# Layer norm and row quantisation of a ternary feed-forward, placed in parts within the DVE's loop, with the rounding on ACT

## The reference, cut to what matters

```python
def act_quant(x):                      # per row
    scale = 128 / jnp.clip(jnp.max(jnp.abs(x), axis=-1, keepdims=True), 1e-5)
    xq = jnp.clip(jnp.round(x * scale), -128, 127) / scale
...
gate = bitlinear(x, w_gate)            # act_quant(x) @ ternary(w_gate).T, 512 -> 2048
up = bitlinear(x, w_up)
intermediate = jax.nn.silu(gate) * up
return h_bitlinear(intermediate, w_down)   # act_quant(fwht(intermediate)) @ ternary(w_down).T
...
x = x + jnp.tanh(g_ffn[1]) * _L1_ffn_ref(_layernorm(x, axis=-1), w_gate, w_up, w_down)
```

## Time and profile before

| | us |
|---|---|
| Median of 3 runs | 3520.1 (3517.28 to 3525.03) |
| Profiled execution | 3514.03 |
| Its span, first to last instruction | 3512.3 |
| PE busy | 3126.2 (89%) |
| DVE busy | 2596.9 (74%) |
| ACT busy | 1831.7 (52%) |
| POOL busy | 1416.7 (40%) |

### The profile page before, as it was taken

The page is one execution under the profiler, slowest core; times in us unless marked ns, Lnnn a source line. Parts: engine busy times, 40 slices in busy tenths (PEclk is TensorE's granted clock), DMA queues, the critical chain, the costliest instruction groups (busy, mean ns, idle before and its releaser), DMA issues. The chain is left out here.

```text
span 3512.3 us, 42714 instructions
## 1 busy us (share of the span) xinstructions
PE 3126.2 (89%) x14213; PEld 1828.2 (52%) x14244; DVE 2596.9 (74%) x3478; ACT 1831.7 (52%) x3430; POOL 1416.7 (40%) x957
## 2 busy tenths in 40 slices
PE   7869798999996888799999999999999788998985
PEld 3337554333333555455555555555555366786663
DVE  7865688877765888478777877787778764766886
ACT  5644343666663556465666566656555342664220
POOL 1122278000000000176777677767767544224430
PEclk9879899999998999899999999999999898999997
DMA  3037745222217200254555454445454356675321
GB/s 133 40 124 274 270 113 139 61 59 62 57 30 167 44 1 1 98 175 156 173 175 169 158 173 160 159 159 181 158 171 137 95 196 214 242 258 192 144 72 60
DMA packets 229749, 478.66 MB, mean 136 GB/s; under 512 B 36239, under 2 KB 69647, under 8 KB 213664
## 3 DMA queue, kind: packets, MB, share of 16 engines
q1 hardware_dynamic: 223296, 459.19, 40.6%
q0 software_dynamic: 6240, 16.81, 1.3%
HBM read 387.51 MB, written 92.06 MB: 137 GB/s over the span
## 5 line engine op out<-in xcount | busy, mean ns | idle before, releaser
L2387 POOL TENSOR_TENSOR l2x_inflow<-l2x_dtu,l2x_rows_b 128x512 f32<-128x512 f32 x256 | 420.1, 1641 | 269.3 <-DVE l2x_state L2276 262.7
L178 POOL TENSOR_TENSOR ln_work<-ln_work,minus_half 128x4 f32<-128x4 f32 (+1 forms) x34 | 33.2, 978 | 1016.1 <-DVE ln_work L166 1016.0
L2276 DVE TENSOR_TENSOR_SCAN l2x_state<-l2x_decay,l2x_inflow 128x512 f32<-128x512 f32 x256 | 384.0, 1500 | 17.0 <-ACT l2x_decay L2150 17.0
L1324 DVE TENSOR_REDUCE l1x_mx<-psum 128x2 f32<-128x1024 f32 x256 | 308.2, 1218 | 97.0 <-PE psum L1166 95.4
L2403 POOL TENSOR_TENSOR l2x_y_sum<-l2x_y_sum,l2x_state 128x512 f32<-128x512 f32 x224 | 354.8, 1584 | 33.0 <-DVE l2x_state L2285 33.0
L2085 ACT ACTIVATE l2x_probs<-psum,l2x_soft,l2x_norms 128x512 f32<-128x512 f32 x256 | 195.7, 775 | 319.1 <-DVE l2x_soft L2215 319.1
L1281 ACT ACTIVATE l1x_split<-psum 128x1024 f32<-128x1024 f32 x256 | 262.1, 1025 | 155.7 <-PE psum L1166 155.7
L2285 DVE TENSOR_TENSOR l2x_state<-l2x_state,l2x_rows_c 128x512 f32<-128x512 f32 x256 | 265.7, 1038 | 6.5
L126 PE MATMUL psum<-l2x_probs_t,l2x_v_tok 128*128 128x512 f32 x512 | 237.3, 607 | 29.1 <-ACT l2x_probs_t L212 26.0
L126 PE MATMUL psum<-l2x_xt,l2x_wq 128*128 128x512 f32 x512 | 231.0, 595 | 7.8 <-issue 6.2
L126 PE MATMUL psum<-l2x_kt,l2x_qt 128*128 128x512 f32 x512 | 230.5, 593 | 4.0 <-ACT l2x_probs L2085 4.0
(11 more groups left out here) (459 smaller groups left out, 7202.3 us busy)
## 6 DMA issues: line engine op xcount, KB each, us to landing
l2x_rows_b<-l3x_xd_dram SPq DMA_DIRECT2D x256, 256.0 KB, 3.5
l2x_rows_c<-l3x_xd_dram SPq DMA_DIRECT2D x256, 256.0 KB, 3.6
l2w_raw<-l_w SPq DMA_DIRECT2D x38, 1024.0 KB, 6.2
l2x_wkv<-l2x_kv_dram SPq DMA_DIRECT2D x32, 1024.0 KB, 6.9
l2w_raw<-l_w SPq DMA_DIRECT2D x38, 512.0 KB, 4.6
l1x_heads_dram<-l1x_stage SPq DMA_DIRECT2D x32, 512.0 KB, 3.3
l2x_wq<-l_wq SPq DMA_DIRECT2D x16, 1024.0 KB, 7.0
l2x_wo<-l_wo SPq DMA_DIRECT2D x16, 1024.0 KB, 5.3
```

Source lines behind the costliest of these rows:

```text
L1324: main.drain(dve.tensor_reduce(mx[:, gg % 2, :, j, t], g["psum"][:, b:b + 2, :], AX.X, ALU.max), f"m{n}_0", banks=2)
L2276: dve.tensor_tensor_scan(state[:, s % KEPT, :], decay[:, s % 3, :], inflow[:, s % 3, :], 0.0, ALU.mult, ALU.add).then_inc(scan_done, 1)
L2387: pool.tensor_tensor(inflow[:, s % 3, :], dtu[:], rows_b[:, s % 3, :], ALU.mult).then_inc(inflow_ready, 1)
```

## The change

`LayerNorm.vector` is split in two, `moments` (statistics, up to what POOL needs) and `apply` (the normalised rows). In phase `l1f` the DVE's loop is put in another order: in each step `widest` comes first, then the extra part of that step, then `rest`, `middle` and `down`. `moments` stands in steps 0, 4, 8, 12, `apply` in steps 1, 5, 9, 13, and `quantise_x` in steps 2, 6, 10. `quantise_x` keeps the maximum and the scales; its two passes over the rows leave the DVE. `x_round` on ACT now multiplies each of the four tiles by its row's scale and adds the rounding constant (four passes over 512 columns), waits for these, and then writes `xq` with a Relu of (top - value), which clips above; the copies to `xqt` turn that back (127 minus the value). `x_round` stands ahead of `y_round` in steps 3, 7, 11. The other parts of the program use `vector` as before.

```diff
--- before.py
+++ after.py
@@ -145,8 +145,12 @@
         self.var_ready, self.rstd_ready, self.xn_ready = [sem(name + n) for n in ("_var_ready", "_rstd_ready", "_xn_ready")]
 
     def vector(self, dve, i, batch, xn_free, xn=None, first=0):
+        self.moments(dve, i, batch, first)
+        xn_free()
+        self.apply(dve, i, batch, xn, first)
+
+    def moments(self, dve, i, batch, first=0):
         g, st = self.g, self.steps
-        xn = g["xn"] if xn is None else xn
         st.begin(i)
         part = slice(first, first + self.tiles)
         stats, w = g["ln_stats"][:, part], g["ln_work"][:, :, part]
@@ -164,7 +168,11 @@
         st.wait(dve)
         dve.tensor_scalar(w[:, 5, :], w[:, 4, :], 1.0 / D, LN_EPS, ALU.mult, ALU.add).then_inc(self.var_ready, 1)
         dve.tensor_scalar(w[:, 6, :], w[:, 3, :], 0.5, None, ALU.mult).then_inc(self.var_ready, 1)
-        xn_free()
+
+    def apply(self, dve, i, batch, xn=None, first=0):
+        g, st = self.g, self.steps
+        xn = g["xn"] if xn is None else xn
+        w = g["ln_work"][:, :, first:first + self.tiles]
         dve.wait_ge(self.var_ready, i * 2 + 2)
         dve.wait_ge(self.rstd_ready, i + 1)
         for s in range(self.tiles):
@@ -1511,6 +1519,7 @@
             sem(n) for n in ("had_in", "x_steps", "z_steps", "x_ready", "xq_done", "mid_ready", "y_scale", "y_rounded", "yq_done", "z_in", "scaled")]
         weight_in = [sem(f"weight_in{k}") for k in range(3)]
         empty_made, emptied, top_made = sem("empty_made"), sem("emptied"), sem("top_made")
+        x_rounded = sem("x_rounded")
         ln = LayerNorm(g, sem)
         blk = ph.block()
         weights = [w_gate, w_up, w_down]
@@ -1612,16 +1621,20 @@
 
             def x_round(b):
                 act.wait_ge(x_ready, b + 1)
+                for s in range(ST):
+                    act.activation(tmp[:, s, :], g["xn"][:, s, :], ACT.Copy, scale=xs[:, b % 2, 2, s:s + 1],
+                                   bias=ROUND).then_inc(x_rounded, 1)
+                act.wait_ge(x_rounded, (b + 1) * ST)
                 if b >= 1:
                     ring.wait_filled(act, 0, f"xq{b - 1}_1")
-                act.activation(xq[:].rearrange("p s d -> p (s d)"), tmp[:].rearrange("p s d -> p (s d)"), ACT.Copy,
-                               bias=-ROUND).then_inc(xq_done, 1)
+                act.activation(xq[:].rearrange("p s d -> p (s d)"), tmp[:].rearrange("p s d -> p (s d)"), ACT.Relu,
+                               scale=-1.0, bias=top[:, 0:1]).then_inc(xq_done, 1)
 
             def x_turned(b):
                 for k in range(2):
                     ring.wait_filled(act, 0, f"xq{b}_{k}")
-                    copy(act, "act", ring, f"xq{b}_{k}", xqt[:, b % 2, 2 * k:2 * k + 2, :].rearrange("p c n -> p (c n)"),
-                         bank_bf(f"xq{b}_{k}"))
+                    ring.drain(act.activation(xqt[:, b % 2, 2 * k:2 * k + 2, :].rearrange("p c n -> p (c n)"),
+                                              bank_bf(f"xq{b}_{k}"), ACT.Copy, scale=-1.0, bias=QMAX), f"xq{b}_{k}")
 
             def middle_turned(t):
                 for n in range(4):
@@ -1660,8 +1673,8 @@
                     ring.wait_filled(act, 0, f"ha{t}_{n}")
                     copy(act, "act", ring, f"ha{t}_{n}", half[:, (n - 2) * BLK:(n - 1) * BLK], bank(f"ha{t}_{n}"))
 
+            act.wait_ge(top_made, 1)
             x_round(0)
-            act.wait_ge(top_made, 1)
             for t in range(T1 + 3):
                 if t % ST == 0 and t < T1:
                     x_turned(t // ST)
@@ -1673,10 +1686,10 @@
                     y_turned(t - 3)
                 if 0 <= t - 1 < T1:
                     halves(t - 1)
+                if t % ST == ST - 1 and t // ST + 1 < NB:
+                    x_round(t // ST + 1)
                 if 0 <= t - 2 < T1:
                     y_round(t - 2)
-                if t % ST == ST - 1 and t // ST + 1 < NB:
-                    x_round(t // ST + 1)
 
         @blk.vector
         def _(dve):
@@ -1696,18 +1709,9 @@
                 xst.wait(dve)
                 xst.inc(dve.reciprocal(v[:, 2, :], v[:, 1, :]))
                 xst.wait(dve)
+                dve.sem_inc(x_ready, 1)
                 dve.tensor_scalar(v[:, 4, :], v[:, 1, :], w_abs[:, 0, 0:1], None, ALU.mult).then_inc(scaled, 1)
                 dve.tensor_scalar(v[:, 5, :], v[:, 1, :], w_abs[:, 0, 1:2], None, ALU.mult).then_inc(scaled, 1)
-                if b >= 1:
-                    dve.wait_ge(xq_done, b)
-                for s in range(ST):
-                    xst.inc(dve.tensor_scalar(tmp[:, s, :], g["xn"][:, s, :], v[:, 2, s:s + 1], QMAX, ALU.mult, ALU.min))
-                xst.wait(dve)
-                for s in range(ST - 1):
-                    xst.inc(dve.tensor_scalar(tmp[:, s, :], tmp[:, s, :], QMIN, ROUND, ALU.max, ALU.add))
-                xst.wait(dve)
-                s = ST - 1
-                dve.tensor_scalar(tmp[:, s, :], tmp[:, s, :], QMIN, ROUND, ALU.max, ALU.add).then_inc(x_ready, 1)
 
             def middle(t):
                 b, s = divmod(t, ST)
@@ -1761,21 +1765,25 @@
 
             quantise_x(0)
             for t in range(T1 + 3):
+                b = t // ST
                 if 0 <= t - 2 < T1:
                     widest(t - 2)
+                if t % ST == 0 and t < T1:
+                    if b == NB - 1:
+                        ring.wait_for(dve, 0, drained=[f"dn{ST - 1}"])
+                    ln.moments(dve, b, (b + 1) % NB)
+                if t % ST == 1 and t < T1:
+                    dve.wait_ge(xq_done, b + 1)
+                    ln.apply(dve, b, (b + 1) % NB)
+                if t % ST == 2 and b + 1 < NB:
+                    ln.wait_xn(dve, b + 1)
+                    quantise_x(b + 1)
+                if 0 <= t - 2 < T1:
                     rest(t - 2)
                 if t < T1:
                     middle(t)
                 if 0 <= t - 3 < T1:
                     down(t - 3)
-                b = t // ST
-                if t % ST == 1 and t < T1:
-                    if b == NB - 1:
-                        ring.wait_for(dve, 0, drained=[f"dn{ST - 1}"])
-                    ln.vector(dve, b, (b + 1) % NB, lambda: dve.wait_ge(x_ready, b + 1))
-                if t % ST == 2 and b + 1 < NB:
-                    ln.wait_xn(dve, b + 1)
-                    quantise_x(b + 1)
 
         @blk.gpsimd
         def _(pool):
```

## The result

| | before | after |
|---|---|---|
| Median | 3521.36 (6 runs, 3517.28 to 3537.24) | 3501.06 (6 runs, 3494.33 to 3515.88) |
| Ratio, with its 95% interval | | 0.9946 [0.9924, 0.9969] |
| Profiled execution, span | 3512.3 | 3514.2 |
| Phase of the ternary feed-forward | 370.8 | 343.3 |

The kernel is faster by 20.3 us (11 to 27 by the interval). I had forecast 32.9 and a time of 3487.2 with a range of 3480 to 3501; the measured 3501.06 is just outside, and the gain is 12.6 short. The profiled execution after is the slowest of its six and no shorter than the one before, so the spans can't be compared. The phase can: from its first row maximum on DVE (1077.82 before, 1095.94 after) to the next phase's first transposes on PE (1448.63 and 1439.21). It lost 27.5 us.

The account below looks back on a forecast made before the run. The order of DVE's work, making PE wait for `widest`, was taken to bound the feed-forward phase. Blocks gain 7.9 + 10.4 + 9.8 + 4.8 = 32.9 us, giving 3487.2 (chance 0.50); range 3484 to 3490, with rivals 3480 to 3501.

Parts of the forecast that it names:

- block 0: First four steps of the feed-forward: `widest` can start earlier, step 3 left as it was; 7.9 us gained.
- block 1: Steps 4 to 7: periods of 21.2, 18.0, 19.2 and 17.3, sum 75.7 against 86.06; 10.4 us gained.
- block 3: Last block, without `quantise_x` or `x_round`: 73.8 against 78.63 us, 4.8 gained.
- the tail and later phases ... move as a whole: Everything after the blocks is behind a barrier and only shifts in time, no gain or loss of its own.
- Stalls of 1 to 3 us stay: PE's waits of this length remain, while the clock cost of the long stalls, 1.5 us each time, goes.
- DVE sets 4k+1 and 4k+2, PE 4k+3: Second to fourth step of each block: 18.0 and 19.2 us from DVE's work plus extra, 17.3 from PE.
- ACT sets step 4k, at 21.2: First step of blocks 1 to 3: `y_round` delays the `xqt` copies by 1.8 us, 19.4 becomes 21.2.
- The clock in step 4k: Rival, chance 0.27: PE's 2.6 us stand for the `xqt` copies lowers its clock, 1.5 us in three blocks; 3491.8.
- The rule against the move to ACT: Skill's rule keeps multiplies and minima on VectorE; the forecast had moving the rounding to ACT pay 1.7 us a block.
- ACT is not in the way: Rival, chance 0.14: copies overlap more or PE catches up, step 4k is DVE's 19.7 us; 3482.7.
- the clock stays low: Rival, chance 0.04: PE stays at low clock through step 4k and the next, 10.6 us more each; 3551, slower.
- the gain is not there: Rival, chance 0.05: PE's third transpose group waits for something else as late, periods stay; 3519.

Follow-up runs that it names:

- spread: Changed kernel with ACT's four scaling passes laid between the SiLU passes of steps 3, 7 and 11; median 3481.1 us, ratio 0.9884 to the kernel before.
- pe_filled: Changed kernel with PE's row transposes of blocks 1 to 3 done three times over into the same banks; median 3493.3 us, ratio 0.9920 to the kernel before.
- order_only: Kernel before with only the new order of DVE's loop, rounding left on DVE and ACT's loop unchanged; median 3502.6 us, ratio 0.9941.
- y_first: Changed kernel with x_round put back behind y_round on ACT; median 3490.0 us, ratio 0.9917 to the kernel before.
- round_only: Kernel before with only the rounding moved to ACT, ahead of y_round, and DVE's old order kept; median 3521.8 us, ratio 1.0009.

## Why the prediction was wrong

By its own steps, with the mean over the six profiled executions of the changed kernel and the two of before (343.0 and 370.9, a gain of 27.9 in the phase):

| term | forecast | measured |
|---|---|---|
| block 0 | 7.9 | 8.2 |
| block 1 | 10.4 | 8.2 |
| block 2 | 9.8 | 7.9 |
| block 3 | 4.8 | 4.2 |
| behind step 16 | 0 | -0.6 |
| phase | 32.9 | 27.9 |
| other phases | 0 | -7.6 by the first medians |
| program | 32.9 | 20.3 by the first medians |

Two steps of the prediction failed. The larger one is "the tail and later phases ... move as a whole": it put everything outside the phase at nothing, and by the medians 7.6 of the 12.6 missing us were lost there. The other is "Stalls of 1 to 3 us stay": it put the fall of the clock in step 4k at nothing, and that cost 3.3. The rest is small: 1.3 in the steps that DVE sets and 0.6 in the tail, with 0.3 more than forecast from block 0.

- *DVE sets 4k+1 and 4k+2, PE 4k+3*: right. The periods are 18.26, 19.46, 17.30 in every execution, within 0.02; the first two are 0.26 more than forecast. In step 4k+1 that is mostly the gap of 0.23 in front of `apply` in the row above; in step 4k+2 I haven't broken it down. Five such periods are 1.3 us.
- *ACT sets step 4k, at 21.2*: right, 21.24 where the clock stays up. The stretch from the first pass to the copies was forecast to a tenth, and `spread` shows that ACT's in-order queue is what made it.
- *The clock in step 4k*: failed. I put "Stalls of 1 to 3 us stay" in the forecast and the fall of the clock at 0.27, priced at 1.5 in three blocks. It fell in 12 of the 18 steps 4k of six executions, at 1.67 each (22.91 less 21.24): 3.3 us an execution. With that rival's price the phase would have been right (28.3 against 27.9); its time, 3491.8, would still have been 9 us under the median.
- *Block 0*: right in sum, by two small misses that cancel. In the first profile `widest` of step 2 began 34.56 behind the row maximum instead of 39.00, and periods of 18.87 and 18.08 followed. I had left step 3 as it was (19.15), and it was 1.1 shorter; the rest came to 7.4 and not 7.9.
- *The tail moves as a whole*: off by 0.6 on the mean; it was 40.1 to 41.7 against 40.6.
- *The phase's gain is the program's*: failed by the medians. The phase gained 27.9 and the medians 20.3 and 19.4, with intervals that end at 27. Two unchanged phases have slow stretches of 16 and 10 us in some executions; they account for the two slowest profiled executions, and they occur with other kernels too (459 with `pe_filled`, 77 with `order_only`, `spread` and the kernel before). The 459 was profiled only in kernels that have the change; of the kernel before there are two profiles, though timed runs of it at 3537 are as far above its median. Whether the changed kernel meets them more often, or the medians of six and nine runs merely drew more of them, or a few us are lost elsewhere, stays open: `y_first` has the same phase and a median of 3490.0. I should have put the scatter of single executions, known from 3517 to 3525 before, into the range beside the rivals.
- *The rule against the move to ACT*: my 1.7 for steps 4k and 4k+2 together holds where the clock stays up: 21.24 + 19.46 = 40.7 against 19.7 + 22.5 = 42.2 in `order_only`, 1.5 less. Where the clock falls it is 42.4, and nothing is left. That sum left out that the last block has only the cost: 72.6 in `order_only` against 74.1 to 75.8 with the rounding on ACT. Over the phase the move pays 3.7 us: 2.8 in block 0 and 2.5 in step 7 of block 1, neither of which I had priced, less 1.8 in the last block. The Trainium skill (ScalarE: Activation LUTs, Rules for kernel authors) would have kept it on VectorE. In one piece on ACT, this case's trace agrees for the last block only. Placed in ACT's idle time (`spread`) the move pays 5.6 and 3.1 us in blocks 1 and 2 and costs nothing in the last, and there the measurement stands against the rule.
- *The range*: its lower end counts 1.8 for ACT's passes, but the 20.7 given for step 4k is 0.5 below 21.2, 1.5 over three blocks. It changes nothing here.

The rivals: *ACT is not in the way* falls by the 2.35 us stall and by `spread`; *the clock stays low* falls, since it was back at 1.00 within the step each time, in all six executions; *the gain is not there* falls by the waits.

## What to carry to other kernels

Free what another engine waits for before doing extra work on an engine that has little time to spare, and spread the extra over the steps that have time left: here the two together made 24 of 28 us, with not one instruction less. They were not run apart. Work moved to another engine pays most where that engine is idle: between its waits the moved passes were worth 12.9 us of the phase, in one piece ahead of something that was due 3.7. When comparing two programs, cut the changed phase out of the trace: it was steady to 2 us where the whole program scattered by 27.

## What the runs showed of the hardware

The same stall of PE doesn't always lower its clock. In step 4k 2.35 us did it in 12 of 18 cases, and in 2 of 3 in `round_only`, each time for exactly two steps of an execution's three; 3.9 us did it in 2 of 3 (`y_first`), 1.10 us in none of 3 (`pe_filled`). The price was 1.67 us behind 2.35, and 2.0 and 1.2 behind 3.9 (24.07 and 23.26 against 22.09). Repeating transposes that nobody needs, in the time of the stall, kept the granted clock at 1.00, 2.4 GHz, in the one profiled execution that has them, and took 3.4 us off the three blocks.

The granted clock can also be low for long in one execution and not in another of the same kernel: 0.72 against 0.95 over the first 105 us of the attention phase, which took 459 instead of 443 us.
